# First stage of a two-layer vision tower: the first layer norm read from PSUM, GpSimd's scaling behind VectorE's distances pass, and VectorE's parts in another order

## The reference, cut to what matters

```python
concat = jnp.concatenate((x, lu, ru, ld, rd), axis=1)            # x and four shifted copies
normed = (concat - mean) * jax.lax.rsqrt(var + EPS)              # one mean and variance per image
normed = normed * gamma[None] + beta[None]
y = conv(normed, W, stride 8) + b                                # 169 tokens of 128 per image

h = _L0_tok_ref(x, ...)
h = h + _L0_attn_ref(_layernorm(h, axis=-1), ...)

def _L0_attn_ref(x, positions, scales, values, W_out, b_out):
    dist_sq = jnp.maximum(x_sq + p_sq[None, None, :] - 2.0 * cross, 0.0)
    dist = jnp.sqrt(dist_sq)
    attn = jax.nn.softmax(scales[None, None, :] / (dist + 0.1), axis=-1)   # 256 positions
    return jnp.einsum('btn,nd->btd', attn, values) @ W_out.T + b_out
```

## Time and profile before

| | |
|---|---|
| runs | 4649.3, 4639.25, 4627.1 us (median 4639.25) |
| profiled execution | 4668.67 us, span 4666.8 us |
| busy in the span | PE 2796.7, DVE 2238.7, ACT 1579.3, POOL 2460.1 us |
| first stage, pipeline over 43 groups | from about 54 us to about 615 us |
| mean granted clock of TensorE | 0.66 of full speed over the span |

### The profile page before, as it was taken

How to read it: one execution, slowest core, us unless ns; L and a number is a source line. 1 busy time by engine, 2 the same in 40 slices (tenths; PEclk the granted TensorE clock), 3 DMA queues, 4 the chain that set the end, 5 groups by cost and what they waited for, 6 DMA issues and landing times. The chain is left out here.

```text
span 4666.8 us, 63125 instructions
## 1 busy us (share of the span) xinstructions
PE 2796.7 (60%) x14076; PEld 2117.4 (45%) x14077; DVE 2238.7 (48%) x7761; ACT 1579.3 (34%) x4281; POOL 2460.1 (53%) x2518
## 2 busy tenths in 40 slices
PE   5888856455545445455454336666666657677663
PEld 4777733233223222232232225655565556566563
DVE  6999965454434444344354333333333333365564
ACT  5777743232222222232222102222222222222221
POOL 5777713445544545435445535555555555565653
PEclk8999965555555555555555557777777776766676
DMA  7777711121221212211112123333333323377774
GB/s 268 248 246 245 245 32 57 61 66 63 67 63 58 63 60 64 65 58 62 61 62 66 61 57 92 94 90 91 84 84 81 84 81 84 106 228 242 237 236 166
DMA packets 401889, 522.45 MB, mean 112 GB/s; under 512 B 65596, under 2 KB 329490, under 8 KB 390514
## 3 DMA queue, kind: packets, MB, share of 16 engines
q1 hardware_dynamic: 318546, 373.60, 26.7%
q0 software_dynamic: 83232, 147.75, 9.3%
HBM read 257.02 MB, written 264.08 MB: 112 GB/s over the span
## 5 line engine op out<-in xcount | busy, mean ns | idle before, releaser
L1089 POOL DMA_INDIRECT xed<-xr,idxs x1014 | 985.9, 972 | 1098.6 <-DVE xr L1671 802.4
L1098 POOL DMA_INDIRECT ytk<-yo,idxy x1080 | 1050.8, 973 | 843.7 <-issue 792.7
L1348 PE MATMUL wide<-wdt,hT 64*128 x2160 | 469.3, 382 | 584.1 <-DVE hT L1839 558.0
L1348 PEld LDWEIGHTS wide<-wdt,hT 64*128 64x128 f32 x2160 | 402.0, 276 | 637.1 <-issue 632.2
L1830 DVE SCALAR_TENSOR_TENSOR ae<-the,bank 128x256 f32<-128x256 f32 x270 | 113.6, 421 | 800.5 <-ACT the L1479 787.7
L1263 PE MATMUL wide<-xn,e 128*128 128x128 f32 (+3 forms) x1024 | 274.9, 392 | 261.9 <-ACT e L1416 247.3
L1488 ACT ACTIVATE yo<-wide,gi 128x128 f32<-128x128 f32 x1080 | 307.3, 370 | 334.1 <-PE wide L1348 183.1
L1330 PE MATMUL bank<-wgu,xeT 128*128 x2160 | 405.4, 350 | 20.2 <-issue 11.3
L1330 PEld LDWEIGHTS bank<-wgu,xeT 128*128 128x128 f32 x2160 | 385.6, 268 | 27.8 <-issue 27.2
L1263 PEld LDWEIGHTS wide<-xn,e 128*128 128x128 f32 (+3 forms) x1024 | 156.9, 202 | 378.2 <-ACT e L1416 261.0
L1473 ACT ACTIVATE xeT<-bank 128x512 f32<-128x512 f32 x270 | 164.4, 609 | 457.2 <-remote 262.6
(11 more groups left out here) (331 smaller groups left out, 5251.8 us busy)
## 6 DMA issues: line engine op xcount, KB each, us to landing
xin<-xed SPq DMA_DIRECT2D x1080, 74.0 KB
ytk<-zeros SPq DMA_DIRECT2D x42, 1536.0 KB, 9.6
yg<-ytk SPq DMA_DIRECT2D x42, 1536.0 KB
xs<-in_xcol SPq DMA_DIRECT2D x42, 1280.0 KB, 6.7
ytk<-yo,idxy POOLq DMA_INDIRECT x1080
xed<-xr,idxs POOLq DMA_INDIRECT x1014
H<-in_ximg SPq DMA_DIRECT2D x4, 2704.0 KB, 22.2
h1d<-H SPq DMA_DIRECT2D x42, 256.0 KB, 9.5
```

Source lines behind the costliest of these rows:

```text
L1089: p.indirect_dma_start(xed[:, :], bass.IndirectOffsetOnAxis(ap=idxs[:, slot, j, k:k + 1], axis=0), xr[:, slot, j, :], None).then_inc(scat[ ...
L1098: p.indirect_dma_start(ytk[:, :], bass.IndirectOffsetOnAxis(ap=idxy[:, slot, j:j + 1], axis=0), yo[:, slot % ES, j, :], None)\
L1348: last = pe.matmul(eO[slot % 2][:, j * D:(j + 1) * D], hT[:, slot % 2, j, :], wdt[:, bass.ds(e, 1), :].rearrange("p o f -> p (o f)"), star ...
```

## The change

- `normalise0` and `stats0` read the convolution's result from its PSUM bank, and no longer ACT's copy in `tok`. The copy is still made, since the residual needs it. As the bank holds the values without the image's factor `rstd`, ACT's Ln takes its square as a scale and Exp its logarithm as a bias; both are computed once into `rstdf`. `conv_x` waits until the norm has read the bank that it writes.
- `scale` works in place on `rr` and waits for `correct` (t_ready), where it waited for `inverse` (r_ready) and the logits before; `logits` reads `rr`.
- `d2` is held twice, so `big` grows from six to seven blocks of 1024 elements. `distance` waits for the logits of a group earlier, and the wait for those of the group before stands ahead of the Exp that writes `rr`.
- On DVE `residual` and the two extremes (now the part `extremes`) come ahead of `logits`.

```diff
--- before.py
+++ after.py
@@ -243,6 +243,7 @@
         part = sb("part", [128, 64])
         mstd = sb("mstd", [128, 2])
         rstd = sb("rstd", [128, 1])
+        rstdf = sb("rstdf", [128, 2])
         mparts = sb("mparts", [128, 3, 2], BF16)
         mrest = sb("mrest", [128, 2])
         mpairs = sb("mpairs", [128, 3, 3, 2])
@@ -263,13 +264,13 @@
         xsq = sb("xsq", [128, 2, TG])
         xh = sb("xh", [128, 2, TG, D])
         xT = sb("xT", [128, TG, D])
-        big = sb("big", [128, 6 * TG * NN])
-        d2, lnr, rr = (big[:, i * TG * NN:(i + 1) * TG * NN].rearrange("p (j n) -> p j n", j=TG) for i in range(3))
-        lg = big[:, 3 * TG * NN:5 * TG * NN].rearrange("p (s j n) -> p s j n", s=2, j=TG)
+        big = sb("big", [128, 7 * TG * NN])
+        lnr, rr = (big[:, i * TG * NN:(i + 1) * TG * NN].rearrange("p (j n) -> p j n", j=TG) for i in range(2))
+        lg, d2 = (big[:, i * TG * NN:(i + 2) * TG * NN].rearrange("p (s j n) -> p s j n", s=2, j=TG) for i in (2, 4))
         mn = sb("mn", [128, 2, TG])
         zz = sb("zz", [128, 2, TG])
         rz = sb("rz", [128, TG])
-        eT = big[:, 5 * TG * NN:6 * TG * NN].rearrange("p (j d) -> p j d", d=128)
+        eT = big[:, 6 * TG * NN:7 * TG * NN].rearrange("p (j d) -> p j d", d=128)
         bst1 = sb("bst1", [128, TG, 6])
         mvs = sb("mvs", [128, TG, 2])
         mv1 = sb("mv1", [128, T, 2])
@@ -305,6 +306,7 @@
         s_psp = sem("s_psp")
         s_ps3 = sem("s_ps3")
         s_v2 = sem("s_v2")
+        s_rstdf = sem("s_rstdf")
 
         def begin_sp(sp):
             w = CH * S * S // 4
@@ -598,9 +600,8 @@
                 def scale(g, slot, rnd):
 
                     nj = tiles_of(g)
-                    p.wait_ge(r_ready, g + 1)
-                    after(p, lg_ready, g)
-                    p.tensor_tensor(lnr[:, 0:nj, :], rr[:, 0:nj, :],
+                    p.wait_ge(t_ready, g + 1)
+                    p.tensor_tensor(rr[:, 0:nj, :], rr[:, 0:nj, :],
                                     scb[:, :].unsqueeze(1).to_broadcast([128, nj, NN]), ALU.mult).then_inc(rs_ready, 1)
 
                 fold(0, 0, 0)
@@ -619,6 +620,7 @@
                     pe.wait_ge(xs_in[slot], 16 * (rnd + 1))
                     pe.wait_ge(weff_ready, g + 1)
                     after(pe, h0_ready, g - 1)
+                    after(pe, xh_ready, g - 1)
                     for j in range(tiles_of(g)):
                         for k in range(NCTX):
                             pe.matmul(psY[slot][:, j * D:(j + 1) * D], xs[:, slot, j, k, :], weff[:, slot, j, k, :],
@@ -701,11 +703,12 @@
 
                     a.wait_ge(mv0, g + 1)
                     nj = tiles_of(g)
-                    a.activation(std[:, slot, 0:nj], mv[:, slot, 0:nj, 1], ACT.Ln, bias=c["eps_ln"][:, :])\
-                        .then_inc(std0, 1)
+                    a.activation(std[:, slot, 0:nj], mv[:, slot, 0:nj, 1], ACT.Ln, scale=rstdf[:, 0:1],
+                                 bias=c["eps_ln"][:, :]).then_inc(std0, 1)
                     a.wait_ge(std0, g + 1)
                     after(a, xsq_ready, g - 1)
-                    a.activation(rs0[:, slot, 0:nj], std[:, slot, 0:nj], ACT.Exp, scale=-0.5).then_inc(rs0_ready, 1)
+                    a.activation(rs0[:, slot, 0:nj], std[:, slot, 0:nj], ACT.Exp, scale=-0.5, bias=rstdf[:, 1:2])\
+                        .then_inc(rs0_ready, 1)
 
                 def copy_xT(g, slot, rnd):
                     a.wait_ge(xt_done, g + 1)
@@ -717,22 +720,22 @@
                     nj = tiles_of(g)
                     a.wait_ge(xsq_ready, g + 1)
                     a.wait_ge(cross_done, g + 1)
-                    after(a, lg_ready, g)
+                    after(a, lg_ready, g - 1)
                     for j in range(nj):
-                        last = a.activation(d2[:, j, :], psD[:, j * NN:(j + 1) * NN], ACT.Relu, bias=xsq[:, slot, j:j + 1])
+                        last = a.activation(d2[:, slot, j, :], psD[:, j * NN:(j + 1) * NN], ACT.Relu, bias=xsq[:, slot, j:j + 1])
                     last.then_inc(d2_ready, 1)
                     a.wait_ge(d2_ready, g + 1)
-                    a.activation(lnr[:, 0:nj, :], d2[:, 0:nj, :], ACT.Ln, bias=tiny[:, :]).then_inc(lnd_ready, 1)
+                    a.activation(lnr[:, 0:nj, :], d2[:, slot, 0:nj, :], ACT.Ln, bias=tiny[:, :]).then_inc(lnd_ready, 1)
                     a.wait_ge(lnd_ready, g + 1)
-                    a.activation(d2[:, 0:nj, :], lnr[:, 0:nj, :], ACT.Exp, scale=0.5).then_inc(dist_ready, 1)
+                    a.activation(d2[:, slot, 0:nj, :], lnr[:, 0:nj, :], ACT.Exp, scale=0.5).then_inc(dist_ready, 1)
 
                 def inverse(g, slot, rnd):
 
                     nj = tiles_of(g)
                     a.wait_ge(dist_ready, g + 1)
+                    a.activation(lnr[:, 0:nj, :], d2[:, slot, 0:nj, :], ACT.Ln, bias=c["tenth"][:, :]).then_inc(ln_ready, 1)
+                    a.wait_ge(ln_ready, g + 1)
                     after(a, lg_ready, g)
-                    a.activation(lnr[:, 0:nj, :], d2[:, 0:nj, :], ACT.Ln, bias=c["tenth"][:, :]).then_inc(ln_ready, 1)
-                    a.wait_ge(ln_ready, g + 1)
                     a.activation(rr[:, 0:nj, :], lnr[:, 0:nj, :], ACT.Exp, scale=-1.0).then_inc(r_ready, 1)
 
                 def probs(g, slot, rnd):
@@ -757,6 +760,9 @@
                 a.wait_ge(s_mstd, 3)
                 a.nop(nofuse=True)
                 a.preload_act_table_set("natural_log_exp_and_others")
+                a.activation(rstdf[:, 0:1], rstd[:, :], ACT.Square).then_inc(s_rstdf, 1)
+                a.activation(rstdf[:, 1:2], rstd[:, :], ACT.Ln).then_inc(s_rstdf, 1)
+                a.wait_ge(s_rstdf, 2)
                 pipeline(a, 0, GA, [(2, distance), (4, copy_eT), (2, inverse), (0, copy_h0), (1, copy_xT), (3, probs),
                                     (0, inverse_std)])
                 a.wait_ge(mv1_ready, GA)
@@ -776,7 +782,7 @@
 
                 def stats0(g, slot, rnd):
                     v.wait_ge(h0_ready, g + 1)
-                    stats(lambda j: tok[:, bass.ds(TG * g + j, 1), :].rearrange("p o d -> p (o d)"), bst,
+                    stats(lambda j: psY[slot][:, j * D:(j + 1) * D], bst,
                           lambda j: mv[:, slot, j, :], tiles_of(g), bn0, mv0, g)
 
                 def normalise0(g, slot, rnd):
@@ -784,7 +790,7 @@
                     after(v, xt_done, g - 1)
                     v.wait_ge(rs0_ready, g + 1)
                     for j in range(nj):
-                        last = v.tensor_scalar(xh[:, slot, j, :], tok[:, bass.ds(TG * g + j, 1), :].rearrange("p o d -> p (o d)"),
+                        last = v.tensor_scalar(xh[:, slot, j, :], psY[slot][:, j * D:(j + 1) * D],
                                                mv[:, slot, j, 0:1], rs0[:, slot, j:j + 1], ALU.subtract, ALU.mult)
                     last.then_inc(xh_ready, 1)
 
@@ -797,7 +803,7 @@
 
                     nj = tiles_of(g)
                     v.wait_ge(r_ready, g + 1)
-                    v.scalar_tensor_tensor(d2[:, 0:nj, :], d2[:, 0:nj, :], 0.1, rr[:, 0:nj, :], ALU.add, ALU.mult)\
+                    v.scalar_tensor_tensor(d2[:, slot, 0:nj, :], d2[:, slot, 0:nj, :], 0.1, rr[:, 0:nj, :], ALU.add, ALU.mult)\
                         .then_inc(t_ready, 1)
 
                 def logits(g, slot, rnd):
@@ -805,7 +811,7 @@
                     v.wait_ge(t_ready, g + 1)
                     v.wait_ge(rs_ready, g + 1)
                     after(v, et_done, g - 1)
-                    v.scalar_tensor_tensor(lg[:, slot, 0:nj, :], d2[:, 0:nj, :], 2.0, lnr[:, 0:nj, :],
+                    v.scalar_tensor_tensor(lg[:, slot, 0:nj, :], d2[:, slot, 0:nj, :], 2.0, rr[:, 0:nj, :],
                                            ALU.subtract, ALU.mult).then_inc(lg_ready, 1)
                     v.wait_ge(lg_ready, g + 1)
                     v.tensor_reduce(mn[:, slot, 0:nj], lg[:, slot, 0:nj, :], AX.X, ALU.min).then_inc(mn_ready, 1)
@@ -821,12 +827,15 @@
                         last = v.scalar_tensor_tensor(t, psO[:, j * D:(j + 1) * D], rz[:, j:j + 1], t, ALU.mult, ALU.add)
                     last.then_inc(h1_ready, 1)
 
-                def stats1(g, slot, rnd):
+                def extremes(g, slot, rnd):
                     nj = tiles_of(g)
                     v.wait_ge(h1_ready, g + 1)
                     here = tok[:, bass.ds(TG * g, nj), :]
                     v.tensor_reduce(hmax[:, bass.ds(TG * g, nj)], here, AX.X, ALU.max)
                     v.tensor_reduce(hmin[:, bass.ds(TG * g, nj)], here, AX.X, ALU.min)
+
+                def stats1(g, slot, rnd):
+                    nj = tiles_of(g)
                     stats(lambda j: tok[:, bass.ds(TG * g + j, 1), :].rearrange("p o d -> p (o d)"), bst1,
                           lambda j: mvs[:, j, :], nj, bn1, mvs_ready, g)
                     v.wait_ge(mvs_ready, g + 1)
@@ -834,7 +843,7 @@
                         .then_inc(mv1_ready, 1)
 
                 statistics(v)
```

(2 more changed lines are left out.)

## The result

Against 4634.7 us before (median of 4 runs, 4627.1 to 4649.3) the changed kernel takes **4570.98 us** (median of 4, 4559.9 to 4576.16); the ratio is 0.9856, 95% interval 0.9824 to 0.9887. On a second chip it was 0.9896 (0.9855 to 0.9937). The forecast was 4569.

The account below looks back on a forecast made before the run. VectorE, partly waiting for GpSimd, was taken to bound the first stage. Steps falling from 12.90 to 11.3 us give 56 us, other terms bring 69.5; from the median 4639.25 that makes 4569 us, range 4543 to 4606.

Parts of the forecast that it names:

- What bounds the kernel: First stage: VectorE sets the 12.90 us step, part of its pace being waits for GpSimd at the norm and distances pass.
- L800: VectorE's distances pass: no longer blocked by GpSimd's scaling, its pitch falls from 1.46 to 1.15 us.
- parts 2 and 3: First stage: GpSimd scales only behind the distances pass; distances are held twice, so ACT needs logits a group earlier.
- L787 from PSUM: First norm on VectorE: reading PSUM frees it from GpSimd, four instructions at 1.13 us against 2.81, -1.7 us a step.
- Stats0: VectorE's statistics for the first norm: reading PSUM instead of SBUF was taken to cost 0.25 us more a step.
- The scaling is hidden: GpSimd's scaling ends 3.65 us after the distances pass starts; VectorE needs it at 5.45, 1.8 us to spare through reordering.
- The step: VectorE's first-stage step: pitches sum to 10.82 us, with 0.3 for a fold and 0.2 for the loop's turn 11.3.
- What is late next: First stage: TensorE, at 11.07 us a step, stands 0.2 us behind VectorE and takes over if VectorE does better.
- The sum: First stage: 56 us from 35 steps, 4.5 from three before, 2.5 from the last three, 6.5 from the opening; 69.5 together.
- (A): Rival: VectorE's residual, with one SBUF operand, is blocked by GpSimd's scaling; step 11.95 us, 4595 us; 13%.
- (B): Rival: the first norm stays tied to GpSimd since it still writes SBUF; step 13.0 us, 4639 us; 7%.
- (C): Rival: nearly always busy, TensorE gets the lower clock; such a step about 22 us, ten of them give 4679; 5%.

Follow-up runs that it names:

- The norm alone: The kernel before with only the norm and stats0 reading PSUM instead of SBUF: ratio to before 1.0004, step 12.92 us.
- xsq was moved: The changed kernel with the two four-column products behind the norm (vr, xsq) made by GpSimd, not VectorE: 4502.55 us, ratio to before 0.9835, step 11.07 us.

## Why the prediction was right, and where not

- **What bounds the kernel** was read wrong. "The stage goes at DVE's pace" took VectorE's fullness for the cause; the ring through ACT and GpSimd set 12.90 us, and VectorE's waiting inside L800 filled its time. The trace of before had it: ACT waited about 0.6 us for the logits in every step, with L603 behind L736 and L800 ending only after L603. The norm alone, at a forecast of -1.7 us, gave nothing. For the whole change this did no harm, since parts 2 and 3 take the scaling and the logits out of the rings; after it, VectorE's sum does set the step, as the sum had assumed: with 0.68 us taken off it, the step fell by 0.75.
- **L787 from PSUM** was right in kind (no wait for GpSimd) and 0.23 us dearer than an L821: 1.36 us for four. **Stats0** was to cost 0.25 us more and costs 0.02: 0.88 against 0.86 us. The two errors work against each other. The rule of the Trainium skill, VectorE: DVE Perf Modes, "The TRN2 errata", has 120 against 58 cycles at 0.96 GHz, which is about 0.06 us more for each instruction from PSUM (an estimate from that page). L793 shows that much (0.40 us against 0.34 free), though not the lost double rate that the prediction added to it; BN_STATS does not (median 282 ns against 276).
- **L800** at a pitch of 1.15: measured 1.15. **The scaling is hidden**: right, it ends at 308.40 and the logits start at 309.94; and the cover is the reordering, as said: without it 1.34 us of wait.
- **The step** is 11.83 us where 11.3 was forecast: the term that was missing is xsq. It has two SBUF inputs, now stands in the folds, and takes 0.54 us instead of 0.16; vr and xsq together 0.68 (302.46 to 303.14) instead of 0.26 (306.94 to 307.20) before:

```profile
307.12 0.16 DVE L794 TENSOR_TENSOR xsq<-vr,rs 128x4 f32<-128x4 f32 x1
307.20 0.17 DVE L816 RECIPROCAL rz<-zz 128x4 f32<-128x4 f32 x1
```

- **The other terms of the step**: L814 waits 0.47 for a fold (0.3 was taken), the norm's pitch is 1.28 and not 1.13, and stats0 gives 0.23 back. That makes a step of 11.62; every second one, where the loop turns, takes 12.11, so the turn costs 0.24 a step (0.2 was taken).
- **What is late next**: TensorE at 11.07 a step, met once xsq was moved. With 0.75 us to TensorE, the changed kernel is not yet at that bound, and the sign "PE and DVE both above 95% busy" failed: from 200 to 500 us they are busy 273.42 and 276.78 of 300.
- **The sum** of 69.5 us stands against 54.5 in the stage: full steps 37.5 (56 forecast), the three before 5.8 (4.5), from group 38 to 42 3.3 (2.5), the opening 7.9 (6.5). The opening's gain is not the change's alone: in the second profile of before it was there without it. By the four pairs of profiles the stage gains 46 to 58 us: 58 with the clock at 1.00 in the opening, 46 with 0.66.
- **The total is right by luck.** The full steps gave 18.5 us less than forecast. The median fell by 63.7 us in the first comparison, of which the interval allows 52 to 82, and by 47.8 on the second chip. The 64 us of the first comparison are beyond what the stage shows; the rest is spread of the runs or lies in `back`, which the change leaves alone, and no run tells which.
- **Rivals.** (A) did not occur: L827 takes 340 to 352 ns beside the scaling, as L821 does alone. (B) did not. (C) neither: from 200 to 500 us the clock is 1.00, also in the version with TensorE at 298.10 of 300 us. It was 0.97 from 160 to 210 us, and 0.91 from 500 to 560, where the folds and convolutions run out and TensorE is busy 48.44 of 60.

## What to carry to other kernels

A full engine need not be the bound (VectorE was busy 93 of 100 us here, and 1.5 us less of work a step gave nothing): when an instruction can be held up after it has started, its waiting is counted as busy, so look for the ring (follow one buffer from engine to engine until it comes back, and add up) before summing the fullest engine. A part of a change can be worth nothing alone and yet be needed (here 0 and 0.53 us a step alone, 1.07 together), so test a change of several edits also edit by edit. Here a tensor_scalar of VectorE that reads PSUM ran beside GpSimd's folds (1.36 us for four), where the same one from SBUF did not (2.36 to 2.89); even a product of four columns with two SBUF inputs took half a microsecond there.

## What was not expected of the hardware

Two four-column products cost 0.68 us a step beside folds, more than half of a 1024-element reduction. The Trainium skill, SBUF — State Buffer, "Who interferes with whom", says that two SBUF inputs contend with a GpSimd instruction that reads SBUF; xsq bears it out. At group 0 of the kernel before, the first L787 was held from 57.17 to 66.24, while thirteen more fold instructions of GpSimd started and ended; in the loop no L787 took more than 0.96 us. Why it was passed over there is open. On one of the chips `back` ran in 2908 us with the same program, against 3928 to 4052 in the profiles on the others, while the first stage kept its step of 12.90 us to 0.01; GpSimd's scatters L1089 there took 982 ns each, against 972 in the first profile, but the idle time before them was 452.4 us in place of 1098.6, and that before the other scatters, L1098, 332.6 in place of 843.7:

```profile
L1089 POOL DMA_INDIRECT xed<-xr,idxs x1014 | 996.0, 982 | 452.4 <-issue 301.5
```

The two differences add up to 1157 us, about the 1144 that `back` is shorter. Why is open.
